# A gated linear recurrence on one Trainium2 core: the 336 steps without a query taken two at a time

## The reference, cut to what matters

```python
bs1 = einsum('bhk,bhkv->bhv', kt, S)
S1  = S + at[..., :, None] * bs1[..., None, :]
S2  = exp(gft)[..., None] * S1
bs2 = einsum('bhk,bhkv->bhv', kt, S2)
S3  = S2 + at[..., :, None] * bs2[..., None, :] + kt[..., :, None] * vt[..., None, :]
o   = einsum('bhk,bhkv->bhv', qt, S3)
out = stack([z, z, o], axis=2).reshape(B, 3 * N, H, HD)[:, -N:]
```

## Time and profile before

| | us |
|---|---|
| median of three executions | 5351.83 |
| profiled execution, its own time | 5317.22 |
| its span, first to last instruction | 5315.1 |
| the recurrence, from `prepare(0)` to the last query | 3391 to 4248 of the span |

### The profile page before, as it was taken

How to read it: one execution, slowest core, us unless ns; L and a number is a source line. 1 busy time by engine, 2 the same in 40 slices (tenths; PEclk the granted TensorE clock), 3 DMA queues, 4 the chain that set the end, 5 groups by cost and what they waited for, 6 DMA issues and landing times.

```text
span 5315.1 us, 115184 instructions
## 1 busy us (share of the span) xinstructions
PE 4435.4 (83%) x43126; PEld 2611.7 (49%) x43126; DVE 3333.7 (63%) x15402; ACT 2603.2 (49%) x5100; POOL 1819.5 (34%) x3734
## 2 busy tenths in 40 slices
PE   5789999999999999984789999778850079999999
PEld 4545555555555555543633437545530044446777
DVE  3287777777777777743066752599999957772111
ACT  1346777777777777751334543444430024453333
POOL 3155666666666666653223220000000022220000
PEclk9879999999999999985878988888875567997999
DMA  4400000000000000002501000010000000000000
GB/s 130 132 10 2 2 12 2 6 8 2 12 2 2 12 2 6 2 2 59 162 7 39 1 1 13 13 26 16 16 17 17 6 6 1 1 1 3 5 5 7
DMA packets 125116, 101.81 MB, mean 19 GB/s; under 512 B 22384, under 2 KB 103568, under 8 KB 124560
## 3 DMA queue, kind: packets, MB, share of 16 engines
q1 hardware_dynamic: 119952, 85.00, 5.8%
q0 software_dynamic: 4608, 9.45, 0.8%
HBM read 74.56 MB, written 19.86 MB: 18 GB/s over the span
## 4 chain that ended last, share of the span: by engine, by line
PE 60%; DVE 20%; ACT 7%; POOL 7%; issue 5%; DMA 1%; SPq 0%; POOLq 0%; DVEq 0%; ACTq 0%; PEldq 0%
PE ps L1731 6%; PE ps L1723 6%; PE ps L1302 5%; PE ps L1342 5%; PE ps L1287 4%; PE ps L1487 4%; PE ps L1499 4%; PE ps L1263 3%; PE ps L1273 3%; PE ps L1528 3%; DVE arena L2822 3%; DVE arena L2802 2%; PE ps L1172 2%; ACT arena L1913 2%; ACT arena L1895 2%
## 5 line engine op out<-in xcount | busy, mean ns | idle before, releaser
L2279 DVE CUSTOM_DVE_ANT_0 arena<-ps,mask_win 128x256 f32<-128x256 f32 (+1 forms) x3072 | 1009.0, 386 | 260.5 <-PE ps L1287 258.8
L1895 ACT ACTIVATE arena<-ps 128x512 f32<-128x512 f32 (+1 forms) x1536 | 752.0, 543 | 575.9 <-PE ps L1302 573.2
L1302 PE MATMUL ps<-arena 32*64 32x384 f32 (+2 forms) x6144 | 748.5, 481 | 73.9 <-ACT arena L1895 73.6
L1287 PE MATMUL ps<-arena 32*64 32x192 f32 (+2 forms) x12288 | 700.7, 326 | 13.0 <-DVE arena L2279 12.6
L1731 PEld LDWEIGHTS ps<-w,arena 128*128 128x128 f32 x4096 | 545.1, 195 | 268.3 <-issue 223.3
L2159 ACT ACTIVATE arena<-ps,eb 128x512 f32<-128x512 f32 x512 | 352.0, 689 | 560.6 <-PE ps L1723 560.5
L2452 DVE CUSTOM_DVE_ANT_0 arena<-ps,mask_cau 128x512 f32<-128x512 f32 (+3 forms) x1024 | 446.5, 487 | 273.1 <-PE ps L1487 270.7
L2012 ACT ACTIVATE arena<-ps 128x512 f32<-128x512 f32 (+2 forms) x768 | 363.6, 526 | 489.6 <-PE ps L1499 489.4
L1731 PE MATMUL ps<-w,arena 128*128 128x128 f32 x4096 | 552.0, 279 | 28.7 <-ACT arena L2159 28.7
L975 POOL TENSOR_SCALAR_AFFINE_SELECT arena<-arena 128x1024 f32<-128x1024 f32 x384 | 420.8, 1096 | 406.2 <-ACT arena L1895 404.5
L1723 PE MATMUL ps<-arena,w 128*128 128x512 f32 x1024 | 534.2, 605 | 0.4
(11 more groups left out here) (331 smaller groups left out, 7953.6 us busy)
## 6 DMA issues: line engine op xcount, KB each, us to landing
w<-in_L_w_dram SPq DMA_DIRECT2D x160, 256.0 KB, 3.3
ys<-arena SPq DMA_DIRECT2D x10, 512.0 KB, 4.8
hs<-arena SPq DMA_DIRECT2D x16, 256.0 KB, 2.3
w<-in_L_w_dram SPq DMA_DIRECT2D x1, 2048.0 KB
scr_k<-arena SPq DMA_DIRECT2D x8, 256.0 KB, 2.3
scr_v<-arena SPq DMA_DIRECT2D x8, 256.0 KB, 2.8
scr_f<-arena SPq DMA_DIRECT2D x8, 256.0 KB, 3.2
arena<-scr_k SPq DMA_DIRECT2D x8, 256.0 KB, 3.6
```

The lines of the kernel that those rows point to most:

```text
L1287: m = pe.matmul(ps[64 * h:64 * h + 64, bank, s.at(v) + lo:s.at(v) + hi], Q[p][r][rows, v, q0:q0 + 64], K[p][r][rows, s.k0 + lo:s.k0 + hi], ...
L1302: m = pe.matmul(out[64 * h:64 * h + 64, :, lo:hi], K[p][r][rows, t.k0 + lo:t.k0 + lo + 64], Q[p][r][rows, 0:2, t.q0 + lo:t.q0 + hi], start ...
L1895: act.activation(PTs[m % L.SLOTS][:, k * w:(k + 1) * w], bank[:, 0:w], exp, scale=-1.0)\
L2279: x = dve.tensor_tensor_reduce(out=seen, in0=bank[:, s.at(v):s.at(v) + s.kw], in1=mask, scale=1.0, scalar=NO_SCORE, op0=ALU.add, op1=ALU.m ...
```

## The change

The 336 unread steps run as 168 pairs (64, 64, 40 and 0 in the four chunks). After `prepare`, a chunk with pairs runs `join_pairs`, 19 instructions over all its pairs at once (1024 or 512 elements in a full chunk), which works out the vectors of two steps in one. A pair is then six instructions: four products with the state (256 elements), the state times both gates (64), the sums (256 to 32), two outer products (128), four rank-one products (256), and a sum over seven terms (448 to 64). The seven terms lie side by side in `J2`, so its writers have a stride of seven floats, 28 bytes. `beside` is called at the same step numbers, but the first sum moves from step 36 to 28, the first product from 60 to 54, the last product from 106 to 108. Steps 336 to 511 run as before; the first of them in chunk 2 has its outer product made ahead of it.

```diff
+    def pairs(self, c):
+        return max(0, min(self.CHUNK, self.QUERIES - self.CHUNK * c)) // 2
...
-        C1 = fw1[:, 32:32 + CH]
+        C1 = LG[:].rearrange("p a b -> p (a b)")[:, 0:CH]
+        J2 = fw1[:, 32:32 + 7 * HD * HD].rearrange("p (a r) -> p a r", r=7)
+        F2 = OQ.rearrange("p t v k -> p (t v k)").rearrange("p (n k) -> p n k", k=HD)
...
+        K2 = take(CH // 2, 2, HD)
+        D2 = take(CH // 2, 3, 2)
...
+        M2 = take(4 * HD, HD)
+        Z2 = take(4, HD)
...
                     chain.link(dve.tensor_tensor(ua, ua, KT, ALU.add))
+                    if R.pairs(c):
+                        join_pairs(c)
                     dve.engine_nop().then_inc(R.pre_done, 1)
+
+                def join_pairs(c):
...
+                    for j, first in enumerate((ua1[:, :, 0], ua1[:, :, 1], kw1[:, :, 0])):
+                        chain.link(dve.tensor_tensor(both, kw2, first.unsqueeze(2).broadcast_to(two), ALU.mult))
+                        chain.link(dve.tensor_reduce(dots[:, :, j], both, AX_X, ALU.add))
+                    chain.add(dve.tensor_copy(key[:, :, 1], kw2[:, :, 0]))
+                    chain.add(dve.tensor_tensor(key[:, :, 0], kw1[:, :, 0], f2, ALU.mult))
+                    chain.link(dve.tensor_tensor(ua1, ua1, f2.unsqueeze(2).broadcast_to(two), ALU.mult))
+                    for a in range(2):
+                        chain.link(dve.tensor_tensor(both, ua2[:, :, a].unsqueeze(2).broadcast_to(two),
+                                                     dots[:, :, 0:2, a].unsqueeze(3).broadcast_to(two), ALU.mult))
+                        chain.link(dve.tensor_tensor(ua1, ua1, both, ALU.add))
+                        chain.link(dve.tensor_tensor(one, ua2[:, :, a], dots[:, :, 2, a].unsqueeze(2)
+                                                     .broadcast_to([P, n, HD]), ALU.mult))
+                        chain.link(dve.tensor_tensor(key[:, :, 0], key[:, :, 0], one, ALU.add))
+                    chain.add(dve.tensor_tensor(kw2, kw2, f1.unsqueeze(2).broadcast_to(two), ALU.mult))
+                    chain.link(dve.tensor_tensor(F2[:, 0:n], f1, f2, ALU.mult))
+
+                def pair(c, at):
+                    q, n, t = c % 2, at // 2, R.CHUNK * c + at
+                    s, new = SH[:, (t - 1) % STEP_RING], SH[:, (t + 1) % STEP_RING]
+                    four = [P, 4, HD, HD]
+                    dve.wait_ge(R.step, t + 1)
+                    chain.add(dve.tensor_tensor(
+                        M2.rearrange("p (a v) k -> p a v k", a=4), s.unsqueeze(1).broadcast_to(four),
+                        KW[q][:, at:at + 2].rearrange("p b a k -> p (b a) k").unsqueeze(2).broadcast_to(four), ALU.mult))
+                    chain.add(dve.tensor_tensor(J2[:, :, 0].rearrange("p (v k) -> p v k", k=HD), s,
+                                                F2[:, n].unsqueeze(1).broadcast_to([P, HD, HD]), ALU.mult))
+                    dve.wait_ge(v_chain, chain.value() - 1)
+                    chain.add(dve.tensor_reduce(Z2.rearrange("p a b -> p (a b)"), M2, AX_X, ALU.add))
+                    chain.add(dve.tensor_tensor(
+                        J2[:, :, 5:7].rearrange("p (v k) r -> p r v k", k=HD),
+                        VT[q][:, at:at + 2].unsqueeze(3).broadcast_to([P, 2, HD, HD]),
+                        K2[:, n].unsqueeze(2).broadcast_to([P, 2, HD, HD]), ALU.mult))
+                    dve.wait_ge(v_chain, chain.value() - 1)
+                    chain.link(dve.tensor_tensor(
+                        J2[:, :, 1:5].rearrange("p (v k) r -> p r v k", k=HD),
+                        UA[q][:, at:at + 2].rearrange("p b a k -> p (b a) k").unsqueeze(2).broadcast_to(four),
+                        Z2.unsqueeze(3).broadcast_to(four), ALU.mult))
+                    dve.tensor_reduce(new.rearrange("p v k -> p (v k)"), J2, AX_X, ALU.add).then_inc(R.step, 2)
...
-                    if at == 36:
+                    if at == 28:
                         add_bank(0, g)
                         stats_of(g)
-                    if at == 60:
+                    if at == 54:
                         silu(g)
                     if at == 86:
                         add_bank(0, g + 1)
                         stats_of(g + 1)
-                    if at == 106:
+                    if at == 108:
                         silu(g + 1)
...
                     if at == 0:
                         prepare(c)
+                    if at < 2 * R.pairs(c):
+                        if at % 2 == 0:
+                            pair(c, at)
+                        beside(c, at)
+                        continue
+                    if at == 2 * R.pairs(c):
                         chain.link(outer(t))
```

More of the change, by code:

```diff
@@ L613, in build @@
         GATE = take(BATCHES, OUT)
+        pair_at = at[0]
         assert at[0] <= rows_at - 2 * TPB * P - 2 * 512
@@ L621, in build @@
         N2, RN, T1 = (frow[:, k, :] for k in range(3))
-        C1 = fw1[:, 32:32 + CH]
+        C1 = LG[:].rearrange("p a b -> p (a b)")[:, 0:CH]
+        J2 = fw1[:, 32:32 + 7 * HD * HD].rearrange("p (a r) -> p a r", r=7)
+        F2 = OQ.rearrange("p t v k -> p (t v k)").rearrange("p (n k) -> p n k", k=HD)
+        at[0] = junk_at
+        K2 = take(CH // 2, 2, HD)
+        D2 = take(CH // 2, 3, 2)
+        assert at[0] <= junk_at + HD * SEEN
+        at[0] = pair_at
+        M2 = take(4 * HD, HD)
+        Z2 = take(4, HD)
+        assert at[0] <= rows_at - 2 * TPB * P - 2 * 512
         G1 = [fw2[:, 2 + q, :] for q in range(2)]
@@ L2756, in prepare @@
                     chain.link(dve.tensor_tensor(ua, ua, KT, ALU.add))
+                    if R.pairs(c):
+                        join_pairs(c)
                     dve.engine_nop().then_inc(R.pre_done, 1)
+                def join_pairs(c):
+                    q, n = c % 2, R.pairs(c)
+                    two = [P, n, 2, HD]
+                    kw = KW[q][:, 0:2 * n].rearrange("p (n b) a k -> p n b a k", b=2)
+                    ua = UA[q][:, 0:2 * n].rearrange("p (n b) a k -> p n b a k", b=2)
+                    f = FT[q][:, 0:2 * n].rearrange("p (n b) k -> p n b k", b=2)
+                    kw1, kw2, ua1, ua2, f1, f2 = kw[:, :, 0], kw[:, :, 1], ua[:, :, 0], ua[:, :, 1], f[:, :, 0], f[:, :, 1]
+                    both = KT[:, 0:2 * n].rearrange("p (n a) k -> p n a k", a=2)
+                    one, key, dots = KT[:, 0:n], K2[:, 0:n], D2[:, 0:n]
+                    for j, first in enumerate((ua1[:, :, 0], ua1[:, :, 1], kw1[:, :, 0])):
[13 more added lines that the diff above has]
+                    chain.link(dve.tensor_tensor(F2[:, 0:n], f1, f2, ALU.mult))
```

## The result

The changed kernel took 5333.22 us (median of 6 executions, 5322.50 to 5346.65) beside 5353.58 us for the kernel before (6 executions of the same session, 5346.14 to 5361.95): a ratio of 0.9949 with a 95% interval of 0.9933 to 0.9965, so 19 to 36 us faster. The forecast was 5319 us, in a range of 5297 to 5348, with faster as the likeliest sign. Sign and range held; the gain in the stage came out smaller than the sum said.

The account below looks back on a forecast made before the run. DVE was taken to bound the 857 us stage, PE not far behind. Terms -89 + 54 + 0.3 + 2 + 1 - 1.6 = -33 us, from the median of 5351.8, gave 5319 us, range 5297 to 5348.

Parts of the forecast that it names:

- unread steps to pairs, with the steps slowed by `newton`: Stage's unread steps on DVE: 168 pairs at 2.29 us for two steps' 2.82, 89 us less; four steps beside `newton` ran slowed.
- `join_pairs`, outer product ahead: Once per chunk with pairs on DVE: 20.0, 20.0 and 13.8 us, 54 in all; outer product at step 336 adds 0.25.
- wait for `newton`, chunks 1 and 2: Ahead of `prepare`: DVE waits about 2 us per chunk for POOL, offset by the slowed steps, net nothing.
- wait at `lengths`: Chunks 0 and 1: 7 pairs, 16 us, replace 17 steps, 24 us, as cover for ACT's reordering; 2 us for the two.
- product of a: DVE comes to it 32.0 us after the sum, with the last sigmoid ready at 32.2; no slack, 1 us in all.
- DVE's waits at the sums: At the first sum DVE still waits 4 us for PE instead of 5.8, a gain of 1.6 us.
- the price of a pair: Six DVE instructions of a pair: 2.10 us without stride cost plus 0.19 for stride, 2.29 us (2.20 to 2.37).
- the gap to the waiting sum: In a pair, between the end of the rank-one products and the start of the sum of 448: 0.04 us.
- The dear-stride rival: Stride-28 writes in pairs 2.1 ns dearer per element: pair 2.91 us, +69 us, 5421; decides at 1.0 ns; chance 0.1 for slower.
- The doubling: Strided pair writes: from 12 to 28 bytes the extra per element doubles by the skill's page to 0.52 ns, 0.20 us a pair.
- The products come too early: At five products DVE waits 3 or 4 us each for sigmoids, 18 us; time 5337, no measurable change; chance 0.17.
- PE sets the pace: With stride free and a pair of 2.10 us, PE's slack limits the stage's gain to 50 us, time 5302; chance 0.13.

Follow-up runs that it names:

- e1: The changed kernel with the three writers of the seven terms writing without a stride (terms in wrong places); stage 814.2 us, pair 2.18 us.
- e7 to e10: Four edits of the runs-of-four kernel: terms in another tensor, eight floats apart, sum over eight, outer products before the 256 sum; stages 821.4, 822.1, 827.2, 830.9 us.
- e3: The changed kernel with vectors reordered once per chunk so rank-one products write runs of four floats; 5310.84 us, ratio 0.9904 to the kernel before, stage 817.0.
- e8: The runs-of-four kernel with terms in another tensor, eight floats (32 bytes) apart instead of seven, sum still over seven; pair 2.22 us, stage 822.1.
- e4: The runs-of-four kernel with the next pair's outer products written ahead of the sum, into a second buffer; pair 2.12 us, stage 815.1.
- e2: The changed kernel with pairs kept but sums and products at the old steps 36, 60, 106; stage 846.4 us, 10.3 more than the changed kernel.

## Why the prediction was right, and where its sum was off

By its own terms, in us of the stage; the measured column adds up starts in the two traces (the unread steps of the kernel before are all 512, 731.3 us, less the 251.5 that the 176 remaining ones take in the changed kernel):

| term | predicted | measured |
|---|---|---|
| unread steps to pairs, with the steps slowed by `newton` | -89 - 4 | -75.8 (479.8 to 404.0) |
| `join_pairs`, outer product ahead | +54.3 | +52.5 |
| wait for `newton`, chunks 1 and 2 | +4 | +3.7 |
| wait at `lengths` | +2 | +2.1 |
| product of a | +1 | 0 |
| DVE's waits at the sums | -1.6 | -3.4 (6.3 to 2.9) |
| wait ahead of one sum of 448 | 0 | +0.5 |
| sum | -33 | -20.4 |

**The step that failed is the price of a pair**, "2.10 us, if writing with 28 bytes of stride cost nothing", plus 0.19 for the stride: 2.29 against 2.41, which is above the prediction's own bounds of 2.20 and 2.37; 168 x 0.12 = 20 us. Two thirds of it is the plain part: e1, without stride, has 2.18 instead of 2.10. I had put "the gap to the waiting sum" at 0.04, from a step's sum, which carries its wait itself; the sum of 448 has the wait as an instruction of its own ahead of it (e7 to e10), so there it is 0.10 to 0.11. The start of each other piece is 0.01 off at most. One third is the stride: 0.23, inside the bounds of 0.10 and 0.27 but nearer to the reading rows than the middle I took. In the other direction, the unread steps that went away had cost 1.428 us on average, not 1.41, which is 2 us in all beyond the 4 that I had counted for `newton`.

**The stride per float** came out at (629 - 418) / 256 = 0.82 ns in the rank-one products, 0.78 in the outer products and in the gates (382 and 272 ns against 282 and 222). That is above both rows from which I bounded it, 0.26 and 0.69. The pair's stride stayed under my upper end only because the gates' extra is hidden entirely and the outer products' all but 0.01 (0.20 to 0.21 from start to start). The dear-stride rival was to decide at 1.0 ns: 0.82 comes near that, but only 256 of its 384 floats weighed on the pair. The Trainium skill's page Advanced Engine Details and Errata, section Memory Cachelines, makes a line of 16 bytes the unit; e3 is in line with it (four floats in a row at the plain price), and so is e8 (single floats at 32 bytes no dearer than at 28). They don't show the line itself: at 28 bytes three of four such runs cross from one line into the next, at no price. The doubling that I read out of it, 0.26 to 0.52, was too small.

**What held.** `join_pairs`: 3447.71 to 3467.26 in chunk 0, 19.55 us, and 19.55 and 13.4 in the next two, against 20, 20 and 14. `prepare(1)` waited 1.87 us for `newton` (predicted about 2):

```profile
3636.14 1.23 DVE L2763 TENSOR_TENSOR arena<-arena,frow 128x1024 f32<-128x1024 f32 x1 [1.87 <-POOLq L1155]
...
3838.75 1.23 DVE L2763 TENSOR_TENSOR arena<-arena,frow 128x1024 f32<-128x1024 f32 x1 [1.87 <-POOLq L1155]
```

The first sum waited 2.9 us for PE (predicted 4). What did not hold are the starts that hung on the pair's price: `prepare(1)` and `prepare(3)` came 198 and 616 us after `prepare(0)`, where the prediction's 3585 and 3995 make it 194 and 604. The row of the first sum:

```profile
3506.30 0.69 DVE L2731 TENSOR_TENSOR X<-ps,X 128x512 f32<-128x512 f32 x1 [2.89 <-PEq L1728]
```

**The rivals.** "The products come too early" didn't happen: DVE's waits for the sigmoids are 8.8 us before and after. Nor is it the dear pair that saved the forecast here: with shorter pairs they are 9.8 (2.18, e1), 7.4 (2.20, e3) and 10.7 us (2.12, e4), far from the rival's 18 more. "PE sets the pace" had its condition, a stride that costs nothing, made true in e1, though with a pair of 2.18 instead of 2.10: the stage then fell to 814.2, 42.4 under the kernel before, where the rival put 50 as the limit. That PE's waits for DVE would be "nearly gone" was wrong for the changed kernel: 46.3 us are left of 63.5, as the stage gave only 20 us.

**Time against stage.** The median fell by 20.4 us, the stage by 20.5; that they agree so closely is luck, as executions of one kernel lie up to 24 us apart. The interval of the ratio, 19 to 36 us, holds the forecast's 33 as well, so the time alone would not have shown that the sum was off; the trace does. That the range held says little about the sum: it would have held with any gain from 6 to 56 us.

## What to carry to other kernels

Price a strided write by the run of floats that stays together, not by the instruction's size: at 28 bytes a single float took some 0.8 ns on top of the plain 1.05, runs of four were free, and turning the operands once per chunk so that the innermost run is four long took 35 us off DVE's pairs for 10 of copies. When two steps of a dependent chain are joined, look in the trace how the new instructions wait: a wait that stands by itself ahead of its instruction cost 0.07 us per pair here, where the old step's sum carried its own. And when an engine speeds up, move what it serves for others by the clock, not by the step: at the old step numbers about half of the gain was lost (e2).

## What the hardware showed that I had not expected

- A DVE instruction that carries its wait itself starts 0.03 us after the end it waits for; with the wait as a separate instruction ahead of it, it starts 0.10 to 0.13 after (168 sums in each of the eleven kernels with pairs, and two of the 22 products for the queries in the kernel before); the statistics there (L2212 and L2216) start 0.15 to 0.17 after. Where the separate wait is over early it costs nothing: 20 steps behind a query's sum have one and start 0.03 after that sum.
- A DVE write of single floats 28 or 32 bytes apart costs about 0.8 ns per float more than a plain one, more than reads at 16 bytes or beyond (0.66 to 0.69) and three times the write at 12 bytes (0.26, L2814).
- What follows the stage, the same code everywhere, took 1051.8 to 1071.7 us over these profiles, without regard to the change; a single execution's time says little here about 10 us.
